# A recommendation tower on one core: every x tile copied wide by DMA, the sums over 16 columns moved to GpSimd

## The reference

```python
x0 = hash_x                                                   # (B, 39, 16)
z0 = einsum('bid,bjd->bdij', x0, x0).reshape(B, D, F0 * F0)
cur0 = relu(einsum('bdk,kl->bld', z0, W0))                    # 128 rows out
next_h, direct0 = split(cur0, 2, axis=1)                      # 64 and 64
z1 = einsum('bid,bjd->bdij', x0, next_h).reshape(B, D, F0 * 64)
cur1 = relu(einsum('bdk,kl->bld', z1, W1))
z = sum(concatenate([direct0, cur1], axis=1), axis=-1)        # over the 16 columns
y = W_top3 . relu(W_top2 . relu(W_top1 . [z, dense_ctx] + b1) + b2)
```

## Time and profile before

| what | value |
|---|---|
| median of 3 runs | 449.19 us (448.59 to 449.31) |
| the profiled execution: its time | 449.96 us |
| its span, first to last instruction | 448.1 us |
| mean granted TensorE clock | 0.97 of full speed |
| TensorE busy | 405.8 us, 91% |
| VectorE busy | 347.6 us, 78% |
| GpSimd busy | 270.8 us, 60% |
| ScalarE busy | 227.2 us, 51% |
| DMA | 64.03 MB moved, mean 143 GB/s |

### The profile page before, as it was taken

The page is one execution under the profiler, slowest core; times in us unless marked ns, Lnnn a source line. Parts: engine busy times, 40 slices in busy tenths (PEclk is TensorE's granted clock), DMA queues, the critical chain, the costliest instruction groups (busy, mean ns, idle before and its releaser), DMA issues.

```text
span 448.1 us, 4257 instructions
## 1 busy us (share of the span) xinstructions
PE 405.8 (91%) x1446; PEld 238.8 (53%) x1446; DVE 347.6 (78%) x197; ACT 227.2 (51%) x224; POOL 270.8 (60%) x180
## 2 busy tenths in 40 slices
PE   0263299999999999999999999999999999999997
PEld 0221056565656565656565565656565656565744
DVE  0301676998989898989898989899898989998900
ACT  2122346556464646465564655655646464645413
POOL 5777888888888888888888888888810000000000
PEclk9958589999999999999999999999999999999999
DMA  8369269493959495868668596959493949752000
GB/s 286 97 152 182 43 145 186 108 213 84 216 117 216 100 205 107 198 136 196 133 155 171 138 193 143 188 125 208 98 211 84 218 96 212 165 129 59 1 0 0
DMA packets 25740, 64.03 MB, mean 143 GB/s; under 512 B 8512, under 2 KB 16661, under 8 KB 19446
## 3 DMA queue, kind: packets, MB, share of 16 engines
q1 hardware_dynamic: 19128, 60.55, 60.4%
q0 software_dynamic: 5632, 1.35, 3.2%
q10 hardware_dynamic: 958, 1.86, 1.2%
HBM read 59.87 MB, written 3.84 MB: 142 GB/s over the span
## 4 chain that ended last, share of the span: by engine, by line
PE 87%; issue 8%; SPq 4%; DMA 0%; ACT 0%
PE acc L495 22%; PE acc L525 14%; PE acc L517 13%; PE acc L518 13%; PE acc L533 12%; PE sums L485 5%; PE spread L506 3%; PE spread L562 2%; SPq L243 1%; SPq L232 1%; SPq L195 1%; SPq L221 0%; PE sums L551 0%; PE sums L553 0%; SPq L205 0%
## 5 line engine op out<-in xcount | busy, mean ns | idle before, releaser
L282 POOL DMA_INDIRECT found<-in_table_dram,rows_sb x176 | 270.6, 1538 | 56.6 <-issue 53.0
L423 DVE TENSOR_TENSOR z_lo<-z,z_hi 128x2048 fp32r<-128x2048 f32 x64 | 146.2, 2285 | 2.3 <-ACT z_hi L325 1.3
L325 ACT ACTIVATE z_hi<-z 128x2048 fp32r<-128x2048 f32 x64 | 122.3, 1911 | 16.8 <-DVE z L415 15.0
L415 DVE TENSOR_TENSOR z<-x_wide,h 128x2048 f32<-128x2048 f32 x48 | 109.8, 2288 | 12.5 <-ACT h L309 8.7
L495 PE MATMUL acc<-squares,w 128*128 128x512 f32 x224 | 114.7, 631 | 0.0
L517 PE MATMUL acc<-z_hi,w_hi 128*128 128x512 f32 x256 | 106.9, 417 | 0.7 <-ACT cur L318 0.7
L518 PE MATMUL acc<-z_hi,w_lo 128*128 128x512 f32 x256 | 100.3, 392 | 0.0
L301 ACT ACTIVATE squares<-sums 128x1024 f32<-128x1024 f32 x64 | 58.8, 919 | 78.7 <-PE sums L485 70.7
L525 PE MATMUL acc<-z_lo,w_hi 128*128 128x512 f32 x256 | 90.5, 475 | 0.0
L415 DVE TENSOR_TENSOR z<-spread,h 128x2048 f32<-128x2048 f32 x32 | 73.1, 2283 | 1.3 <-PE spread L506 1.2
L525 PEld LDWEIGHTS acc<-z_lo,w_hi 128*128 128x128 f32 x256 | 47.0, 188 | 32.3 <-issue 26.8
(11 more groups left out here) (41 smaller groups left out, 111.2 us busy)
## 6 DMA issues: line engine op xcount, KB each, us to landing
x_wide<-x_rows SPq DMA_DIRECT2D x96, 512.0 KB
x_parts<-x_rows SPq DMA_DIRECT2D x62, 64.0 KB
found<-in_table_dram,rows_sb POOLq DMA_INDIRECT x176
w_sb<-in_w_dram SPq DMA_DIRECT2D x1, 1280.0 KB, 7.2
x_rows<-found_hi SPq DMA_DIRECT2D x32, 26.8 KB
x_rows<-found SPq DMA_DIRECT2D x32, 26.8 KB
x_rows<-found_lo SPq DMA_DIRECT2D x30, 26.8 KB
z<-in_select_dram ACTq DMA_DIRECT2D x1, 576.0 KB, 7.9
```

Of the source, the lines that this page charges most:

```text
L282: pool.indirect_dma_start(out=found[:, b, s * D:s * D + D], out_offset=None, in_=table, in_offset=bass.IndirectOffsetOnAxis(ap=rows_sb[:, ...
L325: nc.scalar.activation(z_hi[:, n % RING], z[:, n % RING], ACT.Copy).then_inc(hi_done, 1)
L415: nc.vector.tensor_tensor(z[:, n % RING], x, h[:, c % 2, :].unsqueeze(1).to_broadcast([P, QUADS, N]), ALU.mult).then_inc(multiplied, 1)
L423: nc.vector.tensor_tensor(z_lo[:, n % RING], z[:, n % RING], z_hi[:, n % RING], ALU.subtract).then_inc(lo_done, 1)
```

## The change

All five groups of layer 1 now take x from `x_wide`, which grows from three to five group buffers; the fields are regrouped in one list, and the spreads on TensorE go. `widen` becomes a function of queue, group and half: SyncE issues the lower halves (partitions 0 to 63) and ScalarE the upper ones (64 to 127). `multiply` waits for both halves. The sums over 16 columns leave VectorE, except the last `reduce1`, and become four additions each on GpSimd, of 256, 128, 64 and 32 columns, with a wait for GpSimd's own result before each of the last three. In GpSimd's program step c holds the 11 gathers of chunk c; from step 5 on `reduce0(c - 5)` stands after the fifth gather, and from step 6 on `reduce1(c - 6)` after the eleventh; five steps without gathers follow. `evict0` and `evict1` keep their waits.

```diff
-SPREAD = [1, 3]
-WIDE = [0, 2, 4]
-SPREAD_FROM = [0, 24, 12, 36]
-WIDE_FROM = [[4, 8], [16, 20], [28, 32]]
+FIELDS = [[0, 4], [8, 12], [16, 20], [24, 28], [32, 35]]
+AHEAD = 5
...
+        def widen(queue, n, half):
+            c, g = n // G, n % G
+            f = FIELDS[g][half]
+            if g == 0:
+                queue.wait_ge(full_out[c % BUFS], 16 * SETS * uses(c))
+            if c:
+                queue.wait_ge(multiplied, n - G + 1)
+            queue.dma_start(x_wide[HALF * half:HALF * half + HALF, g, :],
+                            x_rows[c % BUFS, 2, f:f + QUADS, :].rearrange("f n -> (f n)").unsqueeze(0)
+                            .to_broadcast([HALF, QUADS * N])).then_inc(wide_in[g], 16)
...
         @block.sync
-            for i in range(len(WIDE)):
-                widen(0, i)
+            widen(sp, 0, 0)
             bring(1)
+            for n in range(1, G):
+                widen(sp, n, 0)
             bring(2)
-            for c in range(CHUNKS - 1):
-                for i in range(len(WIDE)):
-                    widen(c + 1, i)
-                if c + BUFS < CHUNKS:
-                    bring(c + BUFS)
+            for n in range(G, G * CHUNKS):
+                widen(sp, n, 0)
+                if n % G == G - 1 and n // G + 2 < CHUNKS:
+                    bring(n // G + 2)
...
         @block.gpsimd
+            def sum_up(src, part, dst, halved, c):
+                x, y = src.rearrange("p (b d) -> p b d", d=D), part.rearrange("p (b d) -> p b d", d=D // 2)
+                nc.gpsimd.tensor_tensor(y, x[:, :, 0:8], x[:, :, 8:16], ALU.add).then_inc(halved, 1)
+                pool.wait_ge(halved, 3 * c + 1)
+                nc.gpsimd.tensor_tensor(y[:, :, 0:4], y[:, :, 0:4], y[:, :, 4:8], ALU.add).then_inc(halved, 1)
+                pool.wait_ge(halved, 3 * c + 2)
+                nc.gpsimd.tensor_tensor(y[:, :, 0:2], y[:, :, 0:2], y[:, :, 2:4], ALU.add).then_inc(halved, 1)
+                pool.wait_ge(halved, 3 * c + 3)
+                return nc.gpsimd.tensor_tensor(dst.unsqueeze(2), y[:, :, 0:1], y[:, :, 1:2], ALU.add)
+            def reduce0(c):
+                pool.wait_ge(evicted0, c + 1)
...
+                sum_up(direct[:, :], part0[:, :], feat_b[0:HALF, c * CB:c * CB + CB], halved0, c).then_inc(reduced0, 1)
+            def reduce1(c):
+                pool.wait_ge(evicted1, c + 1)
...
+                sum_up(cur1[:, :], part1[:, :], feat_a[:, c * CB:c * CB + CB], halved1, c).then_inc(reduced1, 1)
...
-            for c in range(CHUNKS):
+            for c in range(CHUNKS + AHEAD):
+                if c >= CHUNKS:
+                    reduce0(c - AHEAD)
+                    reduce1(c - AHEAD - 1)
+                    continue
...
                 for s in range(SLOTS):
+                    if s == SLOTS // 2 and c >= AHEAD:
+                        reduce0(c - AHEAD)
                     pool.indirect_dma_start(
...
+                if c > AHEAD:
+                    reduce1(c - AHEAD - 1)
...
         @block.scalar
                     if n + 1 < G * CHUNKS and is_v(n + 1):
                         high_part(n + 1)
+                    if n + 1 + G < G * CHUNKS:
+                        if n == 0:
+                            widen(act, G, 1)
+                        widen(act, n + 1 + G, 1)
...
         @block.vector
-                if g in SPREAD:
-                    dve.wait_ge(spread_done, len(SPREAD) * c + SPREAD.index(g) + 1)
-                    x = spread[:, :, :]
-                else:
-                    dve.wait_ge(wide_in[WIDE.index(g)], 32 * (c + 1))
-                    x = x_wide[:, WIDE.index(g), :].rearrange("p (t n) -> p t n", n=N)
+                dve.wait_ge(wide_in[g], 32 * (c + 1))
...
-                    if g == 1 and c:
-                        reduce1(c - 1)
-                    if g == G - 1 and c + 1 < CHUNKS:
-                        reduce0(c + 1)
...
         @block.tensor
-            def spread_out(n):
...
-                    if (n + 2) % G in SPREAD and SPREAD[0] < n + 2 < G * CHUNKS:
-                        spread_out(n + 2)
```

More of the change, by code:

```diff
@@ L100, in build @@
         x_rows = nc.dram_tensor("x_rows", (BUFS, 3, F, N), F32, kind="Internal")
-        x_wide = sb("x_wide", [P, len(WIDE), QUADS * N])
+        x_wide = sb("x_wide", [P, G, QUADS * N])
         x_parts = sb("x_parts", [P, BUFS, N], F32R)
-        select_sb = sb("select_sb", [P, T0 + len(SPREAD), P], F32R)
+        select_sb = sb("select_sb", [P, T0, P], F32R)
         w0 = sb("w0", [P, T0, P])
@@ L130, in build @@
         y_sb = sb("y_sb", [1, B])
-        spread = ps("spread", [P, QUADS, N])
+        dense_acc = ps("dense_acc", [P, QUADS, N])
         sums = ps("sums", [P, 2, N])
@@ L138, in build @@
         hid2 = [z[:, 0, m, :] for m in range(M2 // P)]
-        hid1_acc = [sums[:, 0, :], sums[:, 1, :], acc0[:, :], spread[:, 0, :]]
-        hid2_acc = [spread[:, 1 + m, :] for m in range(M2 // P)]
-        y_acc = spread[0:1, 3, :]
+        hid1_acc = [sums[:, 0, :], sums[:, 1, :], acc0[:, :], dense_acc[:, 0, :]]
+        hid2_acc = [dense_acc[:, 1 + m, :] for m in range(M2 // P)]
+        y_acc = dense_acc[0:1, 3, :]
         early, late = slice(0, B - CB), slice(B - CB, B)
@@ L162, in build @@
         full_out = [sem(f"full_out_{b}") for b in range(BUFS)]
-        wide_in = [sem(f"wide_in_{i}") for i in range(len(WIDE))]
+        wide_in = [sem(f"wide_in_{g}") for g in range(G)]
         summed = sem("summed")
@@ L355, in _ @@
                 square(d)
+                if d == 0:
+                    widen(act, 0, 1)
             split(1)
             evict0(0)
+            widen(act, 1, 1)
             high_part(0)
+            for g in range(2, G):
+                widen(act, g, 1)
             square(ND)
@@ L424, in low_part, with reduce1 @@
                                         ALU.subtract).then_inc(lo_done, 1)
[L426 to L432, removed]
+            def reduce1():
+                c = CHUNKS - 1
                 dve.wait_ge(evicted1, c + 1)
@@ L497, in contract0 @@
                 last.then_inc(contracted0, 1)
-            def spread_out(n):
[L501 to L504, removed]
-                    rows = slice(32 * q, 32 * q + 32)
-                    last = nc.tensor.matmul(spread[:, q, :], select_sb[rows, T0 + i, :], x_parts[rows, c % BUFS, :],
-                                            start=True, stop=True)
-                last.then_inc(spread_done, 1)
             def contract1_hi(n):
@@ L581, in _ @@
             pe.wait_ge(w0_ready, 3)
-            spread_out(SPREAD[0])
             for d in range(ND):
@@ L651, in layout @@
     from_w1 = np.asarray(inputs["L0_rec_W1"]).reshape(F, HALF, P)
-    for i, g in enumerate(SPREAD):
-        for q in range(QUADS):
-            for a in range(2):
-                f = SPREAD_FROM[q] + 2 * i + a
-                if f < F:
-                    row = 32 * q + 2 * (f - QSTART[q])
-                    select[row:row + 2, T0 + i, HALF * a:HALF * a + HALF] = 1.0
-                    w1[HALF * a:HALF * a + HALF, QUADS * g + q] = from_w1[f]
-    for i, g in enumerate(WIDE):
-        for a in range(2):
-            f = WIDE_FROM[i][a]
-            w1[HALF * a:HALF * a + HALF, QUADS * g:QUADS * g + QUADS] = from_w1[f:f + QUADS].transpose(1, 0, 2)
+    for g, (f0, f1) in enumerate(FIELDS):
+        for a in range(QUADS):
+            w1[0:HALF, QUADS * g + a] = from_w1[f0 + a]
+            if f1 + a >= f0 + QUADS:
+                w1[HALF:P, QUADS * g + a] = from_w1[f1 + a]
     def by_tile(a):
```

36 lines of the change are left out of this document (15 added, 21 removed).

## The result

Measured: **557.98 us** (median of 4 runs, 555.81 to 559.35) against 449.02 (4 runs, 448.59 to 449.31) on the same chip; ratio 1.2412, 95% interval 1.2384 to 1.244. The profiled execution has a span of 555.6 us. Ratios with an interval leave out executions that came out over 1.5% above the fastest of their kernel.

A forecast was written before the change was run, and what follows sets the result against it. GpSimd was taken to bound ten iterations at 28.7 us a step: 396.0 to iteration 11, then 126.9 with TensorE bounding and 2 at the end, span 524.9, plus 1.1 for the median: 526 us; range 492 to 562, its own 508 to 545.

The forecast's parts named there:

- rival 1: x copies: lower and upper halves do not overlap, iterations 11 to 14 take 27.5 each, 19 us more, 545 us; chance 0.22.
- VectorE holds GpSimd: GpSimd's step: nine two-input SBUF operations of VectorE hold gathers up, 1.15 us each, 10.4 per step.
- Rival 3: GpSimd's gathers: VectorE does not hold them up at all, step 18.3, TensorE bounds, 449 us; chance 0.03.
- Additions at 0.5 each: GpSimd's step: eight additions at 0.5 us each, 4.0 per step, 2.0 per sum.
- Rival 2: GpSimd's additions: almost free at 0.10 each, 492 us (chance 0.08), or dear at 0.99, 567 us (chance 0.07).
- The start: First evict0: evict0(1) waits for 60 gathers and a sum, at 96.6 us instead of 72.82; evict0(2) at 123.3.
- The step of 28.7: GpSimd per iteration: gathers 14.3, holding 10.4 and additions 4.0 make 28.7 us against TensorE's 22.8.
- SyncE's lay-outs stand behind the copies of the same groups as before: SyncE's queue: lay-outs keep their place behind the copies, listed among what costs nothing.
- The last iterations: Iteration 11 to the end: TensorE bounds again, 126.9 us after 396.0, plus 2 at the early MLP.
- 0 to 3.3 lost, I take 2: Early MLP at the end: waits for a cur1 sum of four additions, done by 420.4 at worst; 2 us taken.
- Spreads gone, TensorE at 22.8: TensorE in the main loop: saves 13.4 us in 32 spread groups, 0.84 per iteration, could run at 22.8.
- TensorE's clock: TensorE standing still some 6 us per iteration may halve its clock, but the slower matmuls have those 6 us as cover.

The follow-up runs named there:

- the kernel with only the sums: The kernel before with the sums moved to GpSimd as in the change, spreads and three wide tiles kept; 544.7 us.
- the kernel with the other halves: Against the two-queue kernel with sums on VectorE: SyncE's half goes to partitions 32 to 95, ScalarE's to 0 to 31 and 96 to 127; 446.67 us, one run.

## Why the prediction was right, and where it was off

526 was forecast and 557.98 came, slower as said. The chain of causes held: ScalarE waits for sums on a GpSimd that VectorE holds up. Two terms were too small, and 557.98 lies above the 508 to 545 that the forecast gave itself. That it is inside the range to 562 is luck, for that end was drawn for rival 1 and for dear additions, and neither explains the miss. Of the 32 us missed, 412.74 - 396.0 = 16.7 had gathered by iteration 11, 14.0 came after it, and 1.3 is the median's distance from the span, 2.4 instead of 1.1.

- *VectorE holds GpSimd*: right. In the step above the eleven gathers took 9.94 + 11.02 = 20.96, 6.7 more than 11 x 1.30, and the sums 8.34, 4.1 more than twice the undisturbed 2.12: 10.8 us lost, where 9 x 1.15 = 10.4 was forecast. Rival 3 is out with that. But a price per operation was right for this kernel only, and partly by luck: in the kernel with only the sums, one step (204.11 to 234.53) lost over 11 us to seven such operations, where the price gives 8.1, and most of it in the additions, which the sum took as undisturbed. The Trainium skill, "SBUF — State Buffer", section "Who interferes with whom", says that a VectorE instruction with two SBUF inputs contends with a GpSimd instruction that reads SBUF; the trace agrees, with an addition of 1.89 us where it is 0.73.
- *Additions at 0.5 each*: right. A sum takes 97.18 - 95.06 = 2.12 us undisturbed, against 2.0. Rival 2 gave a sum 0.4 or 4.0, and both are out for additions by themselves; the 8.34 us of two held sums comes near its dear end, but by the hold, which is counted above. The estimate from the Trainium skill, "GPSIMD Engine Reference", section 3.1, 1.05 us per sum, was half of what the trace shows.
- *The start*: 96.6 forecast, 97.02; the second, 123.3, was 123.75. One detail was wrong: the wait stands ahead of direct, behind h, which had gone at 78.86, so VectorE got one more multiply, at 80.10, before it stood still.
- *The step of 28.7*: too small by 1.9. One term of it, "SyncE's lay-outs stand behind the copies of the same groups as before", was costed at nothing. The order in the queue is what it was, but the lay-outs now leave later: SyncE waited 60.7 us for them, 0.5 in the kernel before, and GpSimd, which may not overwrite found until they have left, 1.15 us of the step above. That goes with the slow copies, not with the second queue: with the sums on VectorE its wait was 134.1 with two queues, 168.6 with one, and none with copies to 128 partitions. With 0.4 more of holding and 0.2 of additions that gives 30.5. But this is only where the time of that one step went. The wait does not set the period: GpSimd's timeline has it between none and 1.6 us, in steps that all took 30.3 to 30.7, and the kernel with only the sums has the same steps without it. What fails is the sum of fixed prices itself: as the traces read, the step is the loop over evict1, the last multiply and the sum of cur1. From evict1(1) at 137.35 on, nine steps at 1.9 more are the first part of the miss.
- *The last iterations*: 128.9 us were forecast from iteration 11 to the end, and it took 555.6 - 412.74 = 142.9. 8.4 of that lie in the last one (510.14 to 541.15, 31.0 us, where the kernel before took 22.6). "0 to 3.3 lost, I take 2" charged four held additions; the early MLP waits for eight, since the sum of the last direct stands ahead of that of cur1 and could start at 504.97 at the earliest. Most of the rest is one long iteration, 29.7 us.

GpSimd's last two sums before the early MLP, first and last addition, and the matmul that waited (it answers to the earlier trace rows):

```profile
504.97 2.21 POOL L278 TENSOR_TENSOR part<-direct 64x256 f32<-64x256 f32 x1 [8.51 <-ACT direct L344]
...
519.73 2.17 POOL L284 TENSOR_TENSOR feat_a<-part 128x32 f32<-128x32 f32 x1
...
522.16 1.94 PE L566 MATMUL sums<-feat_b,wt1b_sb 80*128 80x480 f32 x2 [6.54 <-POOL feat_a L284]
```

- *Rival 1, the halves do not overlap*: its mechanism is true, 219 GB/s with two queues against 215, and 27.9 us per iteration where GpSimd is out of the way. By the rule of the Trainium skill, "SBUF — State Buffer", section "Can I just issue two DMAs to hit both halves?", that was to be expected, and the trace agrees. Yet here it cost at most 7 us, not 19: of iterations 11 to 14 (23.2, 22.6, 29.7 and 21.9) one was long. Whether the halves made it long is not shown, for the kernel with the other halves, whose copies are faster, has one of 29.3 too. The copies run up to a chunk ahead, which may be why it was only one; that was not tried.
- *Spreads gone, TensorE at 22.8*: right, 23.0 where nothing else bounds (the copies to 128 partitions), but in the changed kernel no one could see it.
- *TensorE's clock*: it fell to 0.89 in the mean, between the levels of 1.2 and 2.4 GHz, under the cover that was named: TensorE stood still for 53.0 of the 275.39 us, 5.9 per iteration.

## What to carry to other kernels

Before work goes to an engine with time to spare, ask who shares SBUF with it and who will then wait for it: 4.2 us of additions per chunk became 7 us per iteration, because each of them and each gather can wait for one whole VectorE operation, and the next evict1 waits for the last of them. Read a DMA's rate by the partitions that one copy goes to. Look at what short transfers stand behind: a second queue saved 56 us with slow copies, but with faster ones, moving all of them out of the lay-outs' queue cost time (461.92 us against 446.67), and copies to 128 partitions did without a second queue. So speed the copies up first. Parts of a change that bound the same iterations do not add up, so try each alone.

## What the runs showed that was not expected

- The hold between VectorE and GpSimd goes both ways: the low part at 363.89, beside additions, took 2.74 us where it takes 2.29.
- With two of nine holding operations gone the step stayed at 30.6 us: GpSimd's time depends on which operations it meets, and the sum of cur1 got through only behind the iteration's last multiply.
- The copies of x moved at 247 GB/s over 140 us when the halves were cut as 32 to 95 and the rest, against 207 for 0 to 63 and 64 to 127.
- A pattern whose outermost dimension was 2 ran the same 94 MB on 2.2 engines, and the kernel took 1755 us.
